# Banded attention stage of a four-layer kernel: written-out steps, maxima over 32 queries times 160 keys, bands read in place

## What is computed

```python
qkv = x @ Wqkv + bqkv                       # x: 1 x 2048 x 128, 16 heads of 8
q, k, v = heads(q), heads(k), heads(v)
scores = jnp.einsum('bhid,bhjd->bhij', q, k) * DH ** -0.5
band = jnp.abs(idx[:, None] - idx[None, :]) <= 64
scores = jnp.where(band[None, None], scores, neg)
attn = jax.nn.softmax(scores, axis=-1)
out = jnp.einsum('bhij,bhjd->bhid', attn, v) ... @ Wout + bout
```

## Time and profile before

| what | us |
|---|---|
| median of 3 runs | 856.33 |
| lowest, highest | 854.08, 858.31 |
| the profiled execution, in all | 861.29 |
| its span in the trace | 859.5 |
| attention, up to the first instruction of the experts | 291.9 |
| the other three layers | 567.6 |

### The profile page before, as it was taken

How to read it: one execution, slowest core, us unless ns; L and a number is a source line. 1 busy time by engine, 2 the same in 40 slices (tenths; PEclk the granted TensorE clock), 3 DMA queues, 4 the chain that set the end, 5 groups by cost and what they waited for, 6 DMA issues and landing times. The chain is left out here.

```text
span 859.5 us, 18332 instructions
## 1 busy us (share of the span) xinstructions
PE 660.1 (77%) x7554; PEld 384.0 (45%) x7554; DVE 525.7 (61%) x1094; ACT 344.9 (40%) x522; POOL 359.2 (42%) x330
## 2 busy tenths in 40 slices
PE   0617888888888279976977498058998988999995
PEld 0302444444445179876876234023333344444442
DVE  8647667676664733342413667869999974406266
ACT  1421433444344573242414552346544536434320
POOL 9202444444444300000001253228999974966530
PEclk9967999999999559997977689669999999999998
DMA  3156552000000364000000640000000000000000
GB/s 76 37 107 108 89 72 32 0 0 0 0 0 2 111 199 100 3 4 2 4 4 5 261 112 0 0 1 0 0 1 0 0 1 1 1 0 1 12 13 25
DMA packets 17327, 29.76 MB, mean 35 GB/s; under 512 B 3248, under 2 KB 13168, under 8 KB 16240
## 3 DMA queue, kind: packets, MB, share of 16 engines
q1 hardware_dynamic: 17264, 28.87, 14.1%
HBM read 24.54 MB, written 4.19 MB: 33 GB/s over the span
## 5 line engine op out<-in xcount | busy, mean ns | idle before, releaser
L474 ACT ACTIVATE pr_exp<-at_psum 128x1024 f32<-128x1024 f32 x68 | 69.6, 1023 | 131.9 <-PE at_psum L559 131.9
L366 DVE TENSOR_REDUCE pr_neg_max<-at_psum 128x4 f32<-128x1024 f32 x68 | 83.2, 1225 | 49.8 <-PE at_psum L541 49.8
L316 POOL TENSOR_SCALAR_AFFINE_SELECT pr_exp<-pr_exp 128x512 f32<-128x512 f32 x68 | 47.1, 692 | 159.0 <-ACT pr_exp L474 159.0
L1493 POOL TENSOR_TENSOR all_phi_b<-all_phi_b,mo_work 128x512 f32<-128x512 f32 x56 | 71.1, 1269 | 43.3 <-ACT mo_work L1699 38.6
L749 POOL TENSOR_TENSOR all_x<-all_x,ff_x_blocks 128x512 f32<-128x512 f32 x3 | 3.8, 1263 | 173.0 <-ACT ff_x_blocks L940 173.0
L1514 PE MATMUL all_psum<-all_phi,mo_xt 128*128 128x512 f32 x128 | 67.1, 651 | 7.3 <-ACT mo_work L1681 5.6
L536 PE MATMUL at_psum<-band_mask,all_ident_bf 128*128 128x512 bf16 x136 | 43.1, 400 | 38.3 <-DVE pr_q_window L359 38.3
L1463 POOL TENSOR_TENSOR mo_work<-mo_work,mo_max 128x1024 f32<-128x1024 f32 x32 | 61.3, 1916 | 22.1 <-DVE mo_max L1755 22.1
L1547 PE MATMUL all_psum<-mo_xt,all_phi_centred 128*128 128x512 f32 x128 | 65.4, 591 | 0.0
L1600 PE MATMUL all_psum<-mo_work,mo_y_slots 128*128 128x512 f32 x128 | 62.5, 595 | 1.8 <-DVE mo_work L1803 1.8
L1699 ACT ACTIVATE mo_work<-all_psum 128x512 f32<-128x512 f32 x64 | 37.7, 601 | 60.6 <-PE all_psum L1547 60.6
(11 more groups left out here) (339 smaller groups left out, 1340.2 us busy)
## 6 DMA issues: line engine op xcount, KB each, us to landing
all_expert_w<-in_expert_w SPq DMA_DIRECT2D x1, 4096.0 KB, 18.3
ff_b_up<-in_b_up SPq DMA_DIRECT2D x1, 2048.0 KB, 10.2
ff_a_up<-in_a_up SPq DMA_DIRECT2D x1, 2048.0 KB, 16.1
ff_w_down<-in_w_down SPq DMA_DIRECT2D x2, 1024.0 KB, 20.5
at_q_stack<-parts_scratch SPq DMA_DIRECT2D x24, 64.0 KB
at_k_stack<-parts_scratch SPq DMA_DIRECT2D x24, 64.0 KB
at_q_stack<-parts_scratch SPq DMA_DIRECT2D x12, 128.0 KB
at_k_stack<-parts_scratch SPq DMA_DIRECT2D x12, 128.0 KB
```

The source lines that it names most:

```text
L316: nc.gpsimd.affine_select(out=e[:, g, :, 0, :], in_=e[:, g, :, 0, :], compare_op=ALU.is_ge, fill=0.0, base=0, pattern=[[0, GH], [-1, P]], ...
L366: nc.vector.tensor_reduce(negm[:, GH * g:GH * g + GH].rearrange("p (u r) -> p r u", r=2), psum[:, SN + 2 * (g % 2):SN + 2 * (g % 2) + 2, : ...
L474: nc.scalar.activation(e[:, g, :, :, :].rearrange("p h j q -> p (h j q)"), psum[:, ST:ST + 2, :].rearrange("p b n -> p (b n)"), ACT.Exp).t ...
L1493: nc.gpsimd.tensor_tensor(tot[:, ch % 2, :], first, ec[:, ch % 2, j, :], ALU.add).then_inc(added, 1)
```

## The change

The whole `attention` function is rewritten; the other layers and their code are as before.

- There is no hardware loop: all 17 steps are written out. `k_window`, `q_window` and `v_window` and their copies are gone, and PE reads the stacks where they lie.
- `natural` works on units of two heads (eight units a step). One product with the identity writes the mask of 2 x 160 columns; then, for each head and each 32 queries, one product of 49 rows, 32 output columns and 160 keys. DVE's maximum is over 160 keys of two heads (320 elements). It runs two steps ahead of `transposed`, in three PSUM banks.
- The negated maxima are three extra rows of `q_stack` (against rows of ones in `k_stack`), put there by two small DMAs a step (`maxima_in`). `transposed` is then four products of 52 rows and 128 columns for two heads, with nothing added before them, in three PSUM banks. The softmax scale goes into the exponential. Both heads of a unit lie on the same half of the partitions.
- The parts go from SBUF to the stacks in one DMA each, without the scratch tensor. The weights come in a channel order that makes this possible. DVE reads q and k from PSUM; the f32 copy on ACT is gone, and ACT writes the m part.
- x comes in three pieces, and statistics, scaling and projection go piece by piece. The values' bias is folded into a bias row that PE adds in the output projection, and this projection goes tile by tile inside the steps, as do its statistics and part of its scaling.
- POOL no longer clears the whole stacks, only their edges.
- 24 products of 512 columns without a reader (`keep_warm`) stand on PE between the projections and the first `natural`.

The diff, cut to its core:

```diff
-                            nc.gpsimd.memset(ks[:, :, :].rearrange("p j n -> p (j n)").bitcast(F32), 0.0)
+                nc.gpsimd.memset(ks[:, :, 0:P], 0.0)
...
-                                    sp.dma_start(stack[p0:p0 + 8, :, pad + r0:pad + r1], rows[half][:, :, r0:r1]).then_inc(stacked[ch], 16)
+                                    sp.dma_start(dst[p0:p0 + DH, :, pad + r0:pad + r1], part[k][64 * half:64 * half + 64, which, r0:r1]).then_inc(stacked[group], 16)
...
+                def maxima_in(w):
+                    sp.wait_ge(mt_ready, w + 1)
+                    for half in range(2):
+                        p0 = 64 * half + PARTS
+                        sp.dma_start(qs[p0:p0 + 3, :, w * P:w * P + P], m_t[24 * half:24 * half + 24, w % 2, :]).then_inc(nm_in[w % 2], 16)
...
+                    nc.tensor.matmul(psum[:, SN + n % 3, 0:2 * WIN].rearrange("p (i k) -> p i k", i=2), c["identb"][:, :], mask[:, :].unsqueeze(1).broadcast_to([P, 2, WIN]), start=True, stop=False)
+                    for i in range(2):
+                        r, j = head(m, i)
+                        rows = slice(64 * r, 64 * r + PARTS)
+                        for q in range(0, P, QC):
+                            k0 = w * P + q
+                            last = nc.tensor.matmul(psum[q:q + QC, SN + n % 3, WIN * i:WIN * i + WIN], qs[rows, j, k0:k0 + QC], ks[rows, j, k0:k0 + WIN], start=False, stop=(i == 1))
...
+                    v.tensor_reduce(nm[:, r, 0, j:j + 2], psum[:, SN + n % 3, 0:2 * WIN].rearrange("p (i k) -> p i k", i=2), AX_X, ALU.max, negate=True).then_inc(sn_free, 1)
...
+                    for i in range(2):
+                        r, j = head(m, i)
+                        rows = slice(64 * r, 64 * r + PARTS + 3)
+                        for b in range(2):
+                            last = nc.tensor.matmul(psum[:, ST + n % 3, 256 * i + P * b:256 * i + P * b + P], ks[rows, j, (w + b) * P:(w + b) * P + P], qs[rows, j, w * P:w * P + P], start=True, stop=True)
...
+                pe.wait_ge(xt_ready, NCH)
+                pe.wait_ge(rest_ready, 2 * NCH)
+                pe.wait_ge(consts, 10)
+                keep_warm(WARM)
```

873 lines of the change are left out of this document (454 added, 419 removed).

## The result

The changed kernel takes 912.8 us (median of four runs, 911.8 to 913.6) and the kernel of before, on the same chip, 857.3 (854.1 to 859.5): a ratio of 1.065, with a 95% interval from 1.061 to 1.069. It is 6.5% slower, and the forecast was 821.1.

What follows compares the result with a forecast made beforehand. PE was taken to set the step (12.0 us before, 11.3 after). Attention: 54 + 169.5 + 5 + 16.8 + 11.4 = 256.7 us instead of 291.9, 35.2 less, so a median of 821.1; range 802 to 843.

Steps and rivals of the forecast that it cites:

- R6: Before the steps: the DVE stall stays whole or `keep_warm` runs at half clock, +5 to +8 us, 826 to 829; 0.45 with forecast.
- the sum: Attention's terms added up: 256.7 us instead of 291.9, so 826.1 for the profiled execution and 821.1 for the median.
- first `natural`: End of the prologue on PE: the first maximum product was to start at 42.3 us instead of 65.2.
- R2: In `transposed`, all on one half, weight loads show: 0.16 us more a unit, 22 in 17 steps, 843 us; chance 0.10.
- The statistics stall of 8.02 us: Before the steps, DVE stood in a 16-element instruction while POOL cleared `q_stack`; 6.0 us of it was to go.
- R5: Column strips of `natural` don't work side by side with rows halved: 0.33 us more a unit, 861 us; chance 0.07.
- the division: In each step, PE's transpose of the result waits for DVE's division: 0.5 us or less, taken as 0.3.
- The DMA wait: PE waits at the third step for the maxima's small DMAs behind the stacks' large ones: 3.4 us.
- The wait at the fourth step: PE waits for the maxima of step 3, whose DMA stands behind the third portion's m part: 2 us.
- R1: Lean step of 10.6 us: strips at 0.133 us, no division wait, no DMA in the way; 805 us; chance 0.17.
- R3: The step stays at 12.06 us, PE's chain set by hand-overs between engines: 829 us; chance 0.12.
- R4: DMA from SBUF to SBUF at 67 GB/s or below, wait 18 us instead of 5: 834 or more; chance 0.09.

Runs made afterwards that it cites:

- the run with the second block: The changed kernel with 24 more whole-array products of 512 columns without a reader right before the steps: 909.9 us, ratio 1.063.
- the same fillers: Changed kernel plus reader-less products in the start's waits (6 in each of three, 30 ahead of the third step): 831.8 to 905.4 us; with the order changed too, 797.8.

## Why the prediction was wrong

**The step that failed** is the one that took the clock over from the rows of before: "The granted clock was 0.99 in the steps; at full clock 512 columns are 0.213 us". All prices of the new step were worked out at that level, and no rival let the steps run at the other; R6 had half clock for `keep_warm` alone. What the runs showed in its place: the granted clock was 0.50 in the 15 steps, and a step took 17.2 us, where the same step took 11.0 in runs that had 1.00. The bill, against the profiled run (913.6 measured, 826.1 by the sum): first `natural` 1.7 us late, the maxima 1.0 longer, 15 steps with their waits 256.4 us instead of 174.5, which is 81.9, the last two steps and the tail 35.0 instead of 28.2, the other layers 3.7 less. The difference is 87.5 us, and 93% of it is in the 15 steps.

**What was seen and not followed.** R2 noted that the products of `transposed` "are all on one half now; before, two halves took turns", and asked only if weight loads would show. They don't: four products take 0.33 us with the change of shape, as the sum had it. But the rows of before said more: eight products in 0.32 us on two halves. The sum paid for the lost half twice over, 4 x 0.32 before and 8 x 0.32 now, without asking if that could be kept. It could: turns and grouping together are worth 2.5 us a step at full clock (11.0 to 8.55).

**What was right.** The statistics stall of 8.02 us is gone (0.20 us), and the first `natural` comes at 44.0 us (42.3). At full clock a unit costs 0.33 + 0.24 + 0.25 = 0.82 us (0.90), the strips work side by side (0.25 for eight with the change of shape, 0.33 expected; R5 is refuted), and a step 11.0 us (11.3). DVE's maximum takes 0.487 us (0.48), ACT's exponential 0.599 (0.58), POOL's selections 0.63. PE waits 0.3 us a step for the division (0.3). The DMA wait exists and is 3.0 us at the third step (3.4), and it was wanted late, after two slow steps. Where the steps ran at full clock, in the run with the second block, it was 6.0 us: the sum had it too short. The wait at the fourth step (2 us) didn't come. From 58 to 84 us, while the stacks are written, the DMAs move 65 to 80 GB/s at a share of 0.51 to 0.60, much as before. R1, R3 and R4 were about sizes that the clock covered over. Two of the prediction's figures don't come out of its own terms: three changes of shape a unit at 0.17 us would give a step of 12.7 us, not 12.1, and 84 us by 16 bodies is 5.2 on POOL, not 5.1; neither moves the forecast.

**What stays open.** The order in which the products are issued decides between the two behaviours: with it changed and the same fillers, the runs lie within 7 us of each other; without it they spread over 74 us. But the change has two parts, the turns between the halves and the grouping of two units, which halves the changes of shape and brings waits for ACT, so that PE is idle for 7% of the time. No run groups two units on one half, so which part holds the clock isn't shown. Why the clock, once low, doesn't come back in steps that keep TensorE busy all the time on half of the rows, and when exactly it falls in them without a wait (196 us in one run, 59 and 188 in another), isn't settled. The runs show that wider `values` and more pauses don't cure it, and that more whole-array columns do so only in some runs and late.
